# GPS layer (GCN, linear attention, expert FFN) on one NeuronCore: 16-bit count matrices, one clear per stored tile, V evictions ahead of the key store

## The chip, the cores and the metric

One Trainium2 chip, one of its NeuronCores. Engines are called PE (TensorE, matrix products), DVE (VectorE), ACT (ScalarE), POOL (GpSimd) and SP (SyncE, which here only issues transfers). The metric is the device time of one execution in microseconds (us), taken as the median of several runs. The kernel before takes 2583.36 us (2581.44 to 2583.81 in 3 runs).

## The reference

3125 nodes with 768 features and 50000 edges, float32. A transformer-like layer:

```python
xn = layernorm(x)
# two GCN convolutions:  out = D^-1/2 (A + I) D^-1/2 (h W^T) + b,  relu between
# A[dst, src] counts edges, D is the in-degree with the self loop
# linear attention over all nodes, 12 heads of 64, 256 random features:
#   q_p, k_p = exp(t @ rf^T - |t|^2 / 2) / 16 ;  kv = k_p^T v ;  out = q_p kv / (q_p . sum k_p)
#   then a projection, a residual on xn, layernorm with gamma and beta
x = x + gcn(gcn(xn)) + attention(xn)
x = x + ffn(layernorm(x))      # 8 experts of width 128, the larger index of the top 2 decides
```

## The kernel before, in words

The nodes are padded to 25 tiles of 128 rows, and these are taken in 5 chunks of 5 tiles. Products in near float32 accuracy are made of three float16 products (high times high, high times low, low times high), written by `mm_split` (L368 to L374, its matmuls all carry line L372).

**The counts.** The adjacency matrix with its counts is not given; the kernel builds it in device memory as two arrays of 3200 x 3200 cells (`cells[0]` and `cells[1]`, L98), here float32, 41 MB each. Each must be cleared first, tile by tile: `clear_tile` (L385) writes 128 x 3200 cells from a zero buffer in on-chip memory, 1600 KB in pieces of 640 elements, and 50 such transfers clear both. Then POOL adds the edges with 392 indirect accumulating transfers of 128 cells each (L711), alternately into the two arrays so that two can be under way. Its first batch of 14 needs only `cells[0]` cleared, the second batch on needs both (L716 to L724).

**Order of the work.** Everything that SP issues goes in a written order through one queue:

- *Prologue.* SP loads the first 5 tiles of x, the random features, 6 weight blocks of 768 KB and the edge lists (L466 to L491). After the normalised tiles are made, it stores each (`store_xn`, L475) and issues two clears behind each store, 10 in all (L497 to L499). Then it loads the first three x tiles of the next chunk (L500 to L501), waits for the edge keys from DVE, stores them (L503), waits for the store, and loads two blocks of keys copied to all partitions (`kb`, L506).
- *Stage 1*, per chunk c (L515 to L549 for SP, `chunk1` at L1681 for PE): PE makes V for 5 tiles, and K for 6 pairs of heads; each pair p is a unit in which exp of the features, sums of K and V and the degree counts are made. Unit number m = 6c + p. In each unit SP loads a key block as soon as DVE has finished its scan (L532 to L535), issues three clears (`CLEAR_FIRST`, `CLEAR_STEP`, L55, L536), stores an xn tile, loads x tiles, and stores and loads one weight block that ACT and DVE split into halves (`presplit_step`, L509; `presplit_hi` on ACT, L306; `presplit_lo` on DVE, L315). PE runs chunks 0 to 3 in a loop of two chunks per iteration, and chunk 4 behind it.
- *Stage 2* (attention for the queries) uses nothing of the counts. POOL's edge transfers run beside it.
- *Stage 3*: the first GCN product of all 25 tiles, then layer 1: for each of the 25 row tiles SP loads `cells[0]` (L596, L609) to `a_in`, POOL adds `cells[1]` to it with an accumulating transfer (L729) and adds the self loops to the diagonal block (L735), ACT makes the float16 high part (L972), DVE the low part (L1391, L1394), and PE multiplies (L1833). The halves are stored to `ahl_dram` for layer 2, which loads them again.
- *Stage 4*: layer 2, routing and the expert FFN.

**The start of stage 1.** PE makes V of tiles 0 and 1 into two PSUM slots. The third needs a slot back, which ACT gives when it has evicted the first (`activation` at L845). ACT first waits for three things:

```python
            act.wait_ge(consts, 2)
            act.wait_ge(vals_clear, 1)
            act.wait_ge(key_stored, 16)
```

`vals_clear` comes from DVE (L1166 to L1171): after the whole chain for the edge keys (L1144 to L1162) it waits until all 5 xn stores have landed (the buffers `vals` and `kv` lie on the same memory as the x tiles), and clears both. `key_stored` is the landing of the key store (the buffer `kh` that `cast_k`, L821, writes lies on the keys).

Of the kernel before, what the change touches and what calls it, by code (L numbers as in the profile page):

```python
# [15 lines left out]
F16 = mybir.dt.float16  # L16
I32 = mybir.dt.int32
ALU = mybir.AluOpType
# [36 lines left out]
CLEAR_FIRST, CLEAR_STEP = 10, 3  # L55
# [34 lines left out]
def build(nc, x, src_row, dst_row, src_col, dst_col, w_qkv, w_proj, b_proj, gamma, beta, rf_t,  # L90
          g1_t, b1, g2_t, b2, ffn_in, ffn_out, out):
    ctx = ExitStack()
    with ctx:
# [4 lines left out]
        cells = [dram(f"cells{k}", [CELLS, 1]) for k in range(2)]  # L98
# [13 lines left out]
        def at(off, *shape, dt=F32):  # L112
            n = int(np.prod(shape))
            if dt == F16:
                ap = arena[:, off:off + (n + 1) // 2].bitcast(F16)[:, 0:n]
            else:
                ap = arena[:, off:off + n]
                if dt != F32:
                    ap = ap.bitcast(dt)
            if len(shape) == 2:  # L120
                ap = ap.rearrange("p (a b) -> p a b", a=shape[0])
            if len(shape) == 3:
                ap = ap.rearrange("p (a b c) -> p a b c", a=shape[0], b=shape[1])
            return ap
# [5 lines left out]
        def small(*shape, dt=F32):  # L130
            n = int(np.prod(shape))
            n = (n + 1) // 2 if dt == F16 else n
            off = s_at[0]
            s_at[0] += n
            assert s_at[0] <= 53000
            return at(off, *shape, dt=dt)
# [5 lines left out]
        iota = small(P, dt=F16)  # L142
        earlier = small(G, G * P)
# [20 lines left out]


        kcol, idx_all, val_all = at(RX, ET), at(WST + 2304, NE, dt=I32), at(WST + 2304 + NE, NE)
        zeros = at(RT + 4 * 3840, 640)
        far = at(RT + 4 * 3840 + 640, SLOTS // P, dt=I32)
# [41 lines left out]
        a_in = [at(RT + NP * u, NP) for u in range(2)]  # L210
# [172 lines left out]
        zero_rows = zeros.rearrange("p (o f) -> p o f", o=1).to_broadcast([P, 5, 640])  # L383

        def clear_tile(eng, k, n):  # L385
            return eng.dma_start(cells_t[k][n].rearrange("p (a f) -> p a f", a=5), zero_rows)  # L386
# [77 lines left out]
        def _(sp):  # L464
# [25 lines left out]
            for i, a in enumerate((src_row, dst_row, src_col, dst_col)):  # L490
                sp.dma_start(eint[2 * i], a).then_inc(edges_in, 16)  # L491
            def clear(first, count):
# [4 lines left out]
            for n in range(TC):  # L497
                store_xn(n)
                clear(CLEAR_FIRST * n // TC, CLEAR_FIRST // TC)  # L499
            for j in range(3):  # L500
                load_x("seen", 1, j)  # L501
# [164 lines left out]
        def _(pool):  # L666
# [5 lines left out]
            made.link(nc.gpsimd.memset(zeros, 0.0))  # L672
            made.link(nc.gpsimd.affine_select(out=ident_end, in_=ident, compare_op=ALU.is_ge, fill=0.0,
                                              base=-(FIRST_LOOP % P), pattern=[[0, P]], channel_multiplier=1))
            made.link(nc.gpsimd.iota(iota, pattern=[[1, P]], base=0, channel_multiplier=0,
# [50 lines left out]
            for n in range(T):  # L726
                own = a_in[n % 2][:, n * P:(n + 1) * P]
                pool.wait_ge(a_ld[n % 2], 16 * (n // 2) + 16)
                pool.dma_start(a_in[n % 2], cells_t[1][n], accum_op=ALU.add, max_dma_last_dim=2 * NP)\  # L729
# [4 lines left out]
                else:  # L734
                    nc.gpsimd.tensor_tensor(own, own, ident_end if n == FIRST_LOOP // P else ident, ALU.add)\  # L735
                        .then_inc(loops, 1)
# [40 lines left out]
        def _(act):  # L777
# [60 lines left out]
            act.wait_ge(key_stored, 16)  # L838
            for c in range(C):
                more = c + 1 < C  # L840
                for t in range(TC):
# [9 lines left out]
                    if t == TC - 2:  # L851
                        cast_k(c, 0)
# [225 lines left out]
        def _(dve):  # L1078
# [64 lines left out]
            dve.wait_ge(consts, 2)  # L1143
            e = Chain(dve, dve_done, links(20))  # L1144
# [21 lines left out]
            dve.wait_ge(xn_st[0], 16 * 3)  # L1166
            dve.wait_ge(xn_st[1], 16 * 2)
            ch = Chain(dve, dve_done, links(2))
            ch.link(nc.vector.memset(kv, 0.0))
            ch.link(nc.vector.memset(vals, 0.0))  # L1170
            dve.sem_inc(vals_clear, 1)  # L1171
            dve.wait_ge(key_stored, 16)
# [869 lines left out]
```

## Time and profile before

| | |
|---|---|
| median of 3 runs | 2583.36 us |
| span of the profiled execution, first to last instruction | 2579.3 us |
| what lies around the span, median less span | 4.1 us |
| PE busy | 2372.9 us (92%) |
| DVE, ACT, POOL busy | 51%, 34%, 32% |
| moved by DMA | 474.24 MB |
| TensorE clock, mean of the span | 0.964 of full |

The profiled execution has no device time of its own beside the span. A group row reads: line, engine, operation, output and input, count, then busy time, mean length of one in ns, idle time of the engine before them and what ended most of it. "SPq" is the issue of a transfer by SP, of which the time is only that of the issue.

### The profile page before, as it was taken

The page shows a single profiled execution, that of the slowest core. Times are in us where ns is not written, and L with a number is a line of the kernel's source. Part 1 is how long each engine was busy: PE and PEld are TensorE (multiplying, and loading weights), DVE is VectorE, ACT ScalarE, POOL GpSimd, SP SyncE. Part 2 cuts the span into 40 slices and gives each one's busy share as a digit, 9 for nine tenths or more (in the row PEclk, how much of TensorE's full clock was granted, in tenths as well). Part 3 has the DMA queues.
Part 4 walks back from the last instruction along what each step waited for, and adds up shares of the span by engine and source line. Part 5 has one row for each costly group of instructions (what it writes and reads, how often), then busy time and mean ns, then how long its engine had stood idle before and what let it go on. Part 6 is the DMA issues. An engine that isn't in the chain of part 4 may idle for free.

```text
span 2579.3 us, 45374 instructions
## 1 busy us (share of the span) xinstructions
PE 2372.9 (92%) x16783; PEld 1607.5 (62%) x16783; DVE 1304.3 (51%) x2843; ACT 872.7 (34%) x1323; POOL 817.4 (32%) x565
## 2 busy tenths in 40 slices
PE   3899889999899999998899999999998899999576
PEld 2686768787666666665565566666664556666365
DVE  5464547564476766766313444544441334444444
ACT  2353436454474654745112222222220001111033
POOL 0002103656677777877610000000000000000265
PEclk9889899999899999999999999999998999999799
DMA  9698977664423233132543999999986655444287
GB/s 389 243 404 286 400 274 247 165 164 115 99 2 62 11 52 61 0 62 7 130 103 110 295 289 302 278 303 274 283 269 237 210 195 173 171 160 157 73 171 129
DMA packets 192199, 474.24 MB, mean 184 GB/s; under 512 B 74864, under 2 KB 81882, under 8 KB 182460
## 3 DMA queue, kind: packets, MB, share of 16 engines
q1 hardware_dynamic: 109996, 381.82, 40.6%
q0 software_dynamic: 71264, 61.03, 18.0%
q10 hardware_dynamic: 10800, 29.50, 3.0%
q8 instruction: 92, 1.51, 0.2%
q14 instruction: 47, 0.39, 0.0%
HBM read 266.99 MB, written 210.77 MB: 185 GB/s over the span
## 4 chain that ended last, share of the span: by engine, by line
PE 71%; ACT 8%; DVE 8%; DMA 6%; issue 4%; SPq 3%; POOL 0%; DVEq 0%; ACTq 0%; POOLq 0%
PE pair L1833 30%; PE pair L372 27%; PE pair L1665 4%; PE pair L1595 2%; PE pair L1645 2%; DVE arena L1297 2%; DVE arena L1299 2%; DVE arena L1303 2%; ACT arena L902 2%; DMA arena<-in_w_qkv 1%; DMA arena<-in_w_proj 1%; PE pair L1977 1%; PE pair L1964 1%; SPq L386 1%; DMA arena<-ahl_dram 1%
## 5 line engine op out<-in xcount | busy, mean ns | idle before, releaser
L372 PE MATMUL pair<-arena 128*128 128x384 f16 (+2 forms) x5760 | 912.9, 320 | 53.4 <-ACT arena L845 29.0
L711 POOL DMA_INDIRECT cells<-arena x392 | 653.5, 1667 | 626.6 <-DMA cells<-arena 501.1
L1833 PE MATMUL pair<-arena 128*128 128x384 f16 x4900 | 819.6, 328 | 27.2 <-DMA arena<-ahl_dram 12.9
L372 PEld LDWEIGHTS pair<-arena 128*128 128x128 f16 (+1 forms) x5760 | 569.5, 99 | 380.2 <-issue 57.3
L1833 PEld LDWEIGHTS pair<-arena 128*128 128x128 f16 x4900 | 475.6, 98 | 337.2 <-issue 14.6
L741 POOL DMA_INDIRECT slots<-arena x25 | 28.9, 1155 | 493.9 <-DVEq L1521 461.3
L1665 PE MATMUL pair<-arena 128*128 128x66 f32 x1200 | 165.3, 283 | 4.6 <-ACT arena L862 4.2
L1665 PEld LDWEIGHTS pair<-arena 128*128 128x128 f32 x1200 | 154.7, 201 | 13.2 <-ACT arena L862 11.0
L862 ACT ACTIVATE arena<-pair,arena 128x256 f32<-128x256 f32 x300 | 124.0, 473 | 60.9 <-PE pair L1645 58.3
L1764 PE MATMUL pair<-arena 128*128 128x320 f32 x480 | 135.2, 435 | 0.0
L1752 PE MATMUL pair<-arena 128*128 128x320 f16 x720 | 113.9, 303 | 19.7 <-DVEq L1306 15.4
L977 ACT ACTIVATE arena<-arena 128x768 f32<-128x768 f32 x25 | 23.4, 936 | 301.7 <-DVE arena L1400 301.7
L1466 DVE SCALAR_TENSOR_TENSOR arena<-pair,arena 128x768 f32<-128x768 f32 x25 | 25.4, 1017 | 195.0 <-PE pair L1833 195.0
L902 ACT ACTIVATE arena<-pair 128x640 f32<-128x640 f32 x120 | 80.7, 696 | 120.5 <-PE pair L1752 119.9
L729 POOL DMA_DIRECT2D arena<-cells x25 | 30.3, 1213 | 283.3 <-DMA arena<-cells 283.3
L1391 DVE TENSOR_TENSOR arena<-arena 128x3200 f16<-128x3200 f32 x25 | 87.3, 3492 | 58.4 <-ACT arena L972 58.4
L1764 PEld LDWEIGHTS pair<-arena 128*128 128x128 f32 x480 | 90.4, 192 | 34.9 <-issue 0.8
L1192 DVE SCALAR_TENSOR_TENSOR arena<-arena 128x128 f16<-128x128 f32 x392 | 109.2, 346 | 4.3 <-DVE arena L1120 4.3
L1752 PEld LDWEIGHTS pair<-arena 128*128 128x128 f16 x720 | 68.7, 99 | 59.5 <-issue 18.8
L735 POOL TENSOR_TENSOR arena<-arena 128x128 f32<-128x128 f32 x24 | 10.1, 421 | 293.2 <-DMA arena<-cells 293.2
L1037 ACT COPY arena<-pair 128x768 f16<-128x768 f16 x25 | 20.0, 799 | 228.4 <-DVE arena L1466 197.3
L1645 PE MATMUL pair<-arena 128*128 128x256 f16 x600 | 93.2, 290 | 0.0
(198 smaller groups left out, 2431.6 us busy)
## 6 DMA issues: line engine op xcount, KB each, us to landing
cells<-arena SPq DMA_DIRECT2D x50, 1600.0 KB, 16.6
arena<-cells SPq DMA_DIRECT2D x25, 1600.0 KB, 10.6
arena<-cells POOLq DMA_DIRECT2D x25, 1600.0 KB, 13.4
ahl_dram<-arena SPq DMA_DIRECT2D x25, 1600.0 KB, 14.1
arena<-ahl_dram SPq DMA_DIRECT2D x25, 1600.0 KB, 7.7
arena<-in_x SPq DMA_DIRECT2D x70, 384.0 KB, 5.2
arena<-key_dram SPq DMA_DIRECT2D x28, 896.0 KB, 5.9
split_w<-arena SPq DMA_DIRECT2D x32, 384.0 KB
```

The lines of the kernel that those rows point to most:

```text
L372: ins = nc.tensor.matmul(dst[half], left(k, a), right(k, b, half), start=start and n == 0, stop=stop and n == 2)
L711: nc.gpsimd.indirect_dma_start(cells[k], bass.IndirectOffsetOnAxis(ap=idx_all[:, m:m + 1], axis=0), val_all[:, m:m + 1], None, bounds_chec ...
L862: ins = nc.scalar.activation(kp_sb[q][:, h * M:(h + 1) * M], bank(4 + q)[:, h * M:(h + 1) * M], ACT.Exp, bias=knorm[:, p % 2, 2 * t + h:2 ...
L902: nc.scalar.activation(qp_sb[:, g, :].rearrange("p (a b) -> p a b", a=2), bank_pair(1 + s), ACT.Exp).then_inc(qp_free[s], 1)
L1192: nc.vector.scalar_tensor_tensor(out=junk[j % 2], in0=kb[p % 2][:, (j // G) * G * P:(j // G + 1) * G * P], scalar=kcol[:, bass.ds(m * EPU ...
L1297: cn.link(nc.vector.scalar_tensor_tensor(halves_of(ln_den[DH:P]), bank_pair(1 + s)[DH:P], 1e-6, halves_of(den[h][DH:P]), ALU.add, ALU.mult))
L1391: nc.vector.tensor_tensor(a_hl[u][:, 1, :], a_in[u], a_hl[u][:, 0, :], ALU.subtract).then_inc(counts_lo, 1)
L1645: ins = nc.tensor.matmul(bank(4 + n % 2)[:, h * M:(h + 1) * M], kh[p % 2][:, h, t * P:(t + 1) * P], weights, start=(h == 0 and m == 0), st ...
L1665: ins = nc.tensor.matmul(bank(6)[:, g * VW:(g + 1) * VW], kp_sb[n % 2][:, h * M + half * P:h * M + (half + 1) * P], vals[:, t, 2 * p + h, ...
L1752: ins = nc.tensor.matmul(pair[1 + s][:, b, 0:HW], w, rows[p % 2][:, h, b * HW:(b + 1) * HW], start=(n == 0), stop=(n == 2))
L1764: ins = nc.tensor.matmul(pair[1 + s][:, b, 0:HW], kvr[:, p, g, :], qp_sb[:, g, b * HW:(b + 1) * HW], start=(half == 0), stop=(half == 1))
L1833: ins = nc.tensor.matmul(pair[u][:, half, 0:HD], a[:, 0, s * P:(s + 1) * P], X[part][:, s, half * HD:(half + 1) * HD], start=(s == 0 and p ...
```

## The change

- `cells`, `zeros`, `a_in` and `val_all` become unsigned 16-bit. All counts are small whole numbers. A clear is now 800 KB in pieces of 1600 elements; the load of a count tile and the accumulating load are 800 KB each.
- One clear instead of two behind each stored tile: 5 in the prologue, and three per unit as before. So `cells[0]` is done with the clears of unit 6 (before: unit 4), and `cells[1]` with those of unit 14 (before: unit 13).
- The self loops are added through a float32 copy: three POOL operations in place of one.
- SP issues two of the x loads of chunk 1 at once, behind the edge lists, and the third behind the first xn store, in place of all three behind the last clear.
- DVE clears `kv` and the two last columns of each head in `vals` before the edge-key chain, not after it, and no longer the whole of `vals`.
- ACT waits for the key store only ahead of the first `cast_k`; DVE no longer waits for it.

```diff
-CLEAR_FIRST, CLEAR_STEP = 10, 3
+CLEAR_FIRST, CLEAR_STEP = 5, 3
-        cells = [dram(f"cells{k}", [CELLS, 1]) for k in range(2)]
+        cells = [dram(f"cells{k}", [CELLS, 1], U16) for k in range(2)]
+        loop, loop_end, own_f = small(P), small(P), small(P)
-        kcol, idx_all, val_all = at(RX, ET), at(WST + 2304, NE, dt=I32), at(WST + 2304 + NE, NE)
-        zeros = at(RT + 4 * 3840, 640)
+        kcol, idx_all, val_all = at(RX, ET), at(WST + 2304, NE, dt=I32), at(WST + 2304 + NE, NE, dt=U16)
+        zeros = at(RT + 4 * 3840, 1600, dt=U16)
-        a_in = [at(RT + NP * u, NP) for u in range(2)]
+        a_in = [at(RT + NP * u, NP, dt=U16) for u in range(2)]
...
-            return eng.dma_start(cells_t[k][n].rearrange("p (a f) -> p a f", a=5), zero_rows)
+            return eng.dma_start(cells_t[k][n].rearrange("p (a f) -> p a f", a=2), zero_rows)
...
                 sp.dma_start(eint[2 * i], a).then_inc(edges_in, 16)
+            for j in range(2):
+                load_x("seen", 1, j)
...
                 store_xn(n)
+                if n == 0:
+                    load_x("seen", 1, 2)
                 clear(CLEAR_FIRST * n // TC, CLEAR_FIRST // TC)
-            for j in range(3):
-                load_x("seen", 1, j)
             sp.wait_ge(key_made, 1)
...
-            made.link(nc.gpsimd.memset(zeros, 0.0))
+            made.link(nc.gpsimd.memset(zeros, 0))
+            made.link(nc.gpsimd.tensor_copy(loop, ident))
+            made.link(nc.gpsimd.tensor_copy(loop_end, ident_end))
...
-                pool.dma_start(a_in[n % 2], cells_t[1][n], accum_op=ALU.add, max_dma_last_dim=2 * NP)\
+                pool.dma_start(a_in[n % 2], cells_t[1][n], accum_op=ALU.add, max_dma_last_dim=NP)\
...
-                    nc.gpsimd.tensor_tensor(own, own, ident_end if n == FIRST_LOOP // P else ident, ALU.add)\
-                        .then_inc(loops, 1)
+                    pool.wait_ge(loops, n)
+                    made.link(nc.gpsimd.tensor_copy(own_f, own))
+                    made.link(nc.gpsimd.tensor_tensor(own_f, own_f, loop_end if n == FIRST_LOOP // P else loop, ALU.add))
+                    nc.gpsimd.tensor_copy(own, own_f).then_inc(loops, 1)
...
             act.wait_ge(vals_clear, 1)
-            act.wait_ge(key_stored, 16)
...
                     if t == TC - 2:
+                        if c == 0:
+                            act.wait_ge(key_stored, 16)
                         cast_k(c, 0)
...
             dve.wait_ge(consts, 2)
+            dve.wait_ge(xn_st[0], 16 * 3)
+            dve.wait_ge(xn_st[1], 16 * 2)
+            ch = Chain(dve, dve_done, links(2))
+            ch.link(nc.vector.memset(kv, 0.0))
+            ch.link(nc.vector.memset(vals[:, :, :, DH:VW], 0.0))
+            dve.sem_inc(vals_clear, 1)
             e = Chain(dve, dve_done, links(20))
...
             dve.sem_inc(kv_free, 1)
-            dve.wait_ge(xn_st[0], 16 * 3)
-            dve.wait_ge(xn_st[1], 16 * 2)
-            ch = Chain(dve, dve_done, links(2))
-            ch.link(nc.vector.memset(kv, 0.0))
-            ch.link(nc.vector.memset(vals, 0.0))
-            dve.sem_inc(vals_clear, 1)
-            dve.wait_ge(key_stored, 16)
```

## Rows read from the trace of the kernel before

**Rows 1.** The page: the chain that ended last, by engine.
```profile
PE 71%; ACT 8%; DVE 8%; DMA 6%; issue 4%; SPq 3%; POOL 0%; DVEq 0%; ACTq 0%; POOLq 0%
```
**Rows 2.** By chunk: PE, PEld, DVE, ACT, POOL busy (count), clock, DMA share, GB/s.
```profile
34.60:193.60 159.00, 129.20 (x960) 100.33 (x960) 83.57 (x277) 57.85 (x111) 0.00 (x0) 0.84 0.87 340
193.60:336.80 143.20, 124.97 (x964) 98.58 (x961) 74.47 (x263) 61.24 (x115) 23.49 (x14) 0.90 0.94 348
336.80:454.00 117.20, 116.51 (x960) 91.51 (x961) 73.00 (x259) 62.33 (x116) 26.82 (x16) 0.97 0.72 245
454.00:569.80 115.80, 114.92 (x961) 90.99 (x962) 75.06 (x261) 62.68 (x115) 68.38 (x41) 0.99 0.63 167
```
**Rows 3.** PE's waits, 45 to 345 us: in total, times, longest.
```profile
PE pair L372 <- ACT arena L845: 29.0, 2, 26.1
PE pair L1600 <- ACT arena L796: 10.4, 3, 4.9
PE pair L372 <- issue: 6.9, 1, 6.9
```
**Rows 4.** Order of time, 33 to 75 us: start, length, engine, line.
```profile
33.73 0.29 DVE L1146 CAST arena<-arena 128x256 f16<-128x256 f32 x1
34.69 14.34 PE L372 MATMUL pair<-arena 128*128 128x384 f16 x72 [3.80 <-DVE arena L297]
...
43.06 0.38 DVE L1161 TENSOR_SCALAR arena<-arena 128x420 f16<-128x420 int32 x1
...
61.08 1.38 DVE L1169 MEMSET arena<- 128x1584 f32 x1 [17.63 <-DMA xn_dram<-arena]
...
73.93 1.70 ACT L845 ACTIVATE arena<-pair,arena 128x768 f32<-128x768 f32 x2 [42.16 <-DMA key_dram<-arena]
...
75.12 25.34 PE L372 MATMUL pair<-arena 128*128 128x384 f16 x144 [26.08 <-ACT arena L845]
```
**Rows 5.** Windows as in rows 2: the prologue, then stretches of stage 1.
```profile
2.00:39.00 37.00, 12.49 (x74) 7.66 (x75) 31.62 (x51) 18.07 (x21) 5.09 (x22) 1.00 1.01 395
137.00:155.00 18.00, 18.00 (x171) 15.78 (x169) 14.13 (x46) 12.92 (x26) 0.00 (x0) 1.00 1.03 406
170.00:187.00 17.00, 17.00 (x99) 15.78 (x100) 9.00 (x30) 7.31 (x16) 0.00 (x0) 0.51 1.03 399
393.00:407.00 14.00, 14.00 (x121) 11.83 (x120) 10.86 (x41) 9.17 (x18) 0.00 (x0) 0.88 1.03 413
```
**Rows 6.** SP's queue: the clears of units 3 and 4.
```profile
155.17 10.20 SPq L386 DMA_DIRECT2D cells<-arena  x3
...
173.48 10.68 SPq L386 DMA_DIRECT2D cells<-arena  x3
```
**Rows 7.** Transfers issued from 104 to 206 us: KB each, median us to landing.
```profile
cells<-arena SPq DMA_DIRECT2D x18, 1600.0 KB, 16.7
arena<-in_w_qkv SPq DMA_DIRECT2D x5, 384.0 KB, 12.3
```
**Rows 8.** POOL, edge transfers and the first count tile of layer 1.
```profile
408.29 1.54 POOL L711 DMA_INDIRECT cells<-arena  x1 [102.56 <-DMA cells<-arena]
...
458.85 1.54 POOL L711 DMA_INDIRECT cells<-arena  x1 [2.01 <-DMA cells<-arena]
...
1293.40 1.55 POOL L711 DMA_INDIRECT cells<-arena  x1 [1.28 <-DMA cells<-arena]
...
1319.53 1.23 POOL L729 DMA_DIRECT2D arena<-cells  x1 [14.72 <-DMA arena<-cells]
```
**Rows 9.** Layer 1: the first count tile on ACT; then one tile from POOL to PE.
```profile
1384.43 2.85 ACT L972 CAST arena<-arena 128x3200 f16<-128x3200 f32 x1
...
1442.81 0.42 POOL L735 TENSOR_TENSOR arena<-arena 128x128 f32<-128x128 f32 x1 [12.25 <-DMA arena<-cells]
...
1449.68 0.19 DVE L1394 COPY arena<-arena 53x128 f16<-53x128 f16 x1
...
1465.83 4.39 PE L1833 MATMUL pair<-arena 128*128 128x384 f16 x26
```

More of the change, by code:

```diff
@@ L17 @@
 I32 = mybir.dt.int32
+U16 = mybir.dt.uint16
 ALU = mybir.AluOpType
@@ L113, in at @@
             n = int(np.prod(shape))
-            if dt == F16:
-                ap = arena[:, off:off + (n + 1) // 2].bitcast(F16)[:, 0:n]
+            if dt in (F16, U16):
+                ap = arena[:, off:off + (n + 1) // 2].bitcast(dt)[:, 0:n]
             else:
@@ L131, in small @@
             n = int(np.prod(shape))
-            n = (n + 1) // 2 if dt == F16 else n
+            n = (n + 1) // 2 if dt in (F16, U16) else n
             off = s_at[0]
@@ L163, in build @@
         pre_raw, pre_out = at(WST, 1032), at(WST + 1032, 2 * 1032, dt=F16)
-        kcol, idx_all, val_all = at(RX, ET), at(WST + 2304, NE, dt=I32), at(WST + 2304 + NE, NE)
-        zeros = at(RT + 4 * 3840, 640)
-        far = at(RT + 4 * 3840 + 640, SLOTS // P, dt=I32)
+        kcol, idx_all, val_all = at(RX, ET), at(WST + 2304, NE, dt=I32), at(WST + 2304 + NE, NE, dt=U16)
+        zeros = at(RT + 4 * 3840, 1600, dt=U16)
+        far = at(RT + 4 * 3840 + 800, SLOTS // P, dt=I32)
         kh = [at(RX + 1200 + CW * u, 2, CW, dt=F16) for u in range(2)]
@@ L380, in all_cleared @@
             eng.wait_ge(cleared[k], 16 * T)
-        zero_rows = zeros.rearrange("p (o f) -> p o f", o=1).to_broadcast([P, 5, 640])
+        zero_rows = zeros.rearrange("p (o f) -> p o f", o=1).to_broadcast([P, 2, 1600])
         def clear_tile(eng, k, n):
-            return eng.dma_start(cells_t[k][n].rearrange("p (a f) -> p a f", a=5), zero_rows)
+            return eng.dma_start(cells_t[k][n].rearrange("p (a f) -> p a f", a=2), zero_rows)
         chain_of, before_group, groups = {}, {}, [0, 0]
```

## The prediction

> **What bounds the kernel now.** I read the chain that ended last first: 71% of it is PE, 6% DMA, 3% SP's queue [rows 1]. So time is to be had where PE waits. Then the busy times cut at the borders of the chunks of stage 1 [rows 2]: chunks 2 and 3 take 117.2 and 115.8 us with PE busy for all but 1 us; chunk 0 takes 159.0 with PE busy for 129.2, chunk 1 143.2 with 125.0, and in these two the DMA engines are busy 87 and 94% of the time. The four chunks do the same work (960 matmuls). So some 42 and 26 us of the first two are stalls and slow clock, and both are rich in DMA. PE's waits name the largest piece: 26.1 us in one wait for ACT's V eviction, 2.9 in a second, 10.4 us for transposes, and one of 6.9 us with no releaser, where PE's loop goes back at 330 us [rows 3].
>
> In order of time [rows 4]: PE finishes V tiles 0 and 1 at 49.0 and stops until 75.1. ACT's first eviction, at 73.9, waited for the key store to land; that store waited behind the prologue's clears in SP's queue; and DVE, done with the edge keys at 43.4, idled 17.6 us until the xn stores had landed. From 2 to 39 us the queue moved 395 GB/s, in the units of chunk 0 about 400, with the DMA engines busy all the time [rows 5]: this is the full rate, and SP falls behind. The clears of unit 3 go out at 155.2, those of unit 4 at 173.5, 18.3 us apart [rows 6], where a unit of chunk 2 takes about 14 us.
>
> **Part by part.**
>
> *The first stall: 26.1 us.* The last xn store lands once all ahead of it is moved. Ahead of it are the weights (6 x 768 KB), 8 x tiles, 5 stores of 384 KB, 1.1 MB of edges and the rest, and now 4 clears of 800 KB: 14.3 MB, where 8 clears of 1600 KB made it 23 MB or more. At 395 GB/s from 2 us on that is 38 us; before, it was 61.1 [rows 4]. DVE reaches that wait at 33.7 (it now stands ahead of the edge chain), idles 5 us, clears `kv` in 1.4 and the two columns in an estimated 0.3, and frees ACT at about 40.5. V tile 0 is done near 43 (the 72 matmuls' 14.3 us fit 16 at 0.32 us, half of full speed, and 56 at 0.163), so its eviction runs at once, and PE passes 49.0 without a stop. Margin: DVE may be 6 us later.
>
> What is queued behind DVE's new wait is the edge chain, 9.7 us long (33.7 to 43.4). It ends at 50.3 in place of 43.4. The key store then meets an empty queue: I take 4 us for it, so `key_stored` is there at 54.5, and the key blocks (two of 896 KB, 4.6 us at 400 GB/s) at 61. `cast_k` needs `key_stored` only after V 2, V 3 and K 0, at 49.0 + 3 x 5.9 = 66.7: covered by 12 us. The x loads of chunk 1 (tiles 3 and 4) go out behind the key blocks and land near 62; statistics end near 65, before DVE is wanted at 68. Without this cover the same few us would come back.
>
> *No second cold start: 1.8 us.* After the stall PE took 25.3 us for 144 matmuls [rows 4]; at 0.163 us each these are 23.5.
>
> *The rest of chunk 0: 11.5 us.* From 75.1 to 193.6 are 118.5 us; the same part of chunk 2 is 117.2 less 12.0 for two V tiles, 105.2. Of the 13.3 too much 1.8 stand above. The rest is a wait of 3.2 us and a stretch from 170 to 187 at granted clock 0.51, half of full speed [rows 5], right behind that wait. Both come from late transfers: a weight block lands 12.3 us after its issue [rows 7], ACT and DVE wait for it in order, and the x tile behind it on DVE is late for PE's transposes. From 104 to 206 us, six units, 18 clears of 1.64 MB went out [rows 7], 29.5 of some 42 MB. Halved they leave 27.3 MB, 4.6 MB a unit, 11.4 us at 400 GB/s, against 14 us of PE's work. SP no longer falls behind. A unit of chunk 2 that ran at DMA share 1.03 kept PE busy all its 14.0 us [rows 5], so short bursts are harmless.
>
> The Trainium skill speaks against this step: "DMA: Bandwidth & Descriptors" (Bandwidth) wants transfers of 1 MiB or more for 75% of peak, and a clear falls from 1.6 MB to 0.8. It has 341 GB/s at 1 MB; as an estimate from it a unit would take 13.4 us or more, and the queue would hardly keep up (the first rival's case). The trace disagrees: the queue of rows 5 held transfers of 384 to 1600 KB and moved 400.
>
> *Chunk 1: 24 us.* It takes 143.2; chunk 2 takes 117.2; the difference is 26.0. In it are the waits of 2.9, 7.2 of the 10.4, 6.9 at the loop's end, and another stretch at half speed. The 6.9 us have no releaser in the trace; they fell in full DMA traffic, and I read them as PE waiting for its instructions to be fetched behind it. I leave 2 us of them (ends 0 and 6.9; nearer to 0, since the queue will be busy four fifths of the time and not all of it).
>
> *Chunk 2: 0.* It now holds nine clears of 0.8 MB where it had four of 1.6.
>
> *Edge transfers: 0.* Their second batch waits for the clears of unit 14, not 13: 14 us later beside PE, less 6 for the shorter landing. So they start at 408.3 - 63 + 8 = 353 and need 885 us for 377 steps [rows 8], 2.35 each: the last at 1238. The first count tile is ready 26 us later (1293.4 to 1319.5 before): 1264, and ACT wants it at 1384.4 [rows 9] - 63 = 1321. Cover 57 us.
>
> *Layer 1: 0.* The count tile for the next row tile is finished on DVE at 1449.9, and PE takes it up at 1465.8 [rows 9]: 16 us of cover. Three POOL operations for one of 0.42 us [rows 9] cost about 1.3 us more with their waits, two transfers of half the bytes give more than that back. Ends: 0, or a loss only if the accumulating load of 16-bit cells took over 16 us more than now. The two extra copies in the prologue and the longer zero buffer (under 1 us) end before SP is wanted at 13.9.
>
> Sum: 26.1 + 1.8 + 11.5 + 24 = 63.4. From the span of 2579.3 that is 2516; with the 4.1 us around it, against the median of 2583.4, **2520 us**.
>
> **Rivals.**
> 1. *Traffic still lags in chunks 0 and 1.* 16-bit transfers move fewer bytes per second, or the late landings have another cause. Then the 35.5 us of the two chunks come by half or less, 0 to 18: 2537 to 2555. For: the clears stay 54% of a unit's bytes. Against: chunks 2 and 3. Chance 0.13.
> 2. *The first stall moves to the xn stores.* If the last store lands not at 38 but near 50, DVE frees ACT 6 us too late and PE stops there; the edge chain, the keys and `cast_k` follow 6 us later inside their cover. 2526 to 2530. Chance 0.07.
> 3. *The edge transfers become the bound* (slower than before). Accumulating into 2-byte cells may land later, and each array's transfers wait for one another. Price: from 408.3 to 458.9 there are 17 steps [rows 8], 2.97 us each, mostly waiting. At that pace for all 377 the last is at 353 + 1120 = 1473, the first tile ready at 1499, 178 late against 1321: 2520 + 178 = 2698. It decides from 2.50 us a step (57/377 more); from 2.67 on the kernel is slower than before. Against: that stretch had much other traffic, and later steps follow POOL's own 1.5 us. Chance 0.03.
> 4. *The change does not free V*: `vals_clear` comes as late as before. Only a wrong reading of the order would do it; 2520 + 26 = 2546. Chance 0.01.
>
> **How the numbers follow.** Forecast 0.76. A measurement of this kernel tells some 0.2% (5 us) from no change. Range: downward the 6.9 us fully gone, chunk 3's pace for chunks 0 and 1, and a little elsewhere, 2508; upward half of the two chunks' gain lost and some of rival 2, 2541. That leaves out the worse part of rival 1 and rival 3. Faster: all but rival 3, 0.96; same 0.01; slower 0.03.
>
> **What would show it.** Right: V evictions from about 43 us on, no PE gap at 49; the last xn store landing near 38, DVE's `kv` clear right behind it; clears of one chunk at the pace of PE's units, 14 us, with weight blocks landing in 4 to 8 us; chunks 0 and 1 near 120 us each; PE at full clock throughout; POOL's second batch from about 353. Wrong: chunks 0 and 1 still over 130 us, a gap at 49, edge steps over 2.5 us, or a longer row tile in layer 1 than now.

## The result and the profile after

The change made the kernel faster: **2524.94 us** median (2520.66 to 2531.73 in four runs) against 2583.59 for the kernel before on the same chip, ratio 0.9779 with a 95% interval of 0.976 to 0.9797. The forecast was 2520.0 in a range of 2508 to 2541. The profiled execution took 2527.59 us, its span is 2525.8, so 1.8 us lie around a span. I had taken 4.1 for that, the median of before less the span of one execution. With 1.8 around it that execution took some 2581.1 us, 2.3 under its median, and the profiled one after is 2.7 above its own. So the spans lie 53.5 us apart and the medians 58.6.

The page of the kernel after: the engines, the DMA total, and the chain by engine, which answers to [rows 1].

```profile
span 2525.8 us, 45448 instructions
...
PE 2350.2 (93%) x16783; PEld 1590.9 (63%) x16783; DVE 1261.0 (50%) x2843; ACT 870.3 (34%) x1323; POOL 866.3 (34%) x615
...
DMA packets 172999, 392.22 MB, mean 155 GB/s; under 512 B 74864, under 2 KB 81882, under 8 KB 166460
...
PE 77%; DVE 8%; ACT 8%; issue 4%; DMA 3%; SPq 0%; POOL 0%; DVEq 0%; ACTq 0%; POOLq 0%
```

SP's queue has left the chain (3% to 0%), DMA has halved in it (6% to 3%), and 82 MB fewer are moved (474.24 less 392.22): the clears of both arrays are 41 MB smaller, and so are the loads of their tiles.

By chunk, against [rows 2] and the first of [rows 5] (length, then PE, PEld, DVE, ACT, POOL busy with counts, granted clock, DMA share, GB/s):

```profile
34.60:152.40 117.80, 117.17 (x960) 91.74 (x960) 80.97 (x279) 58.42 (x112) 0.00 (x0) 0.99 0.74 263
152.40:274.50 122.10, 114.67 (x962) 91.27 (x960) 74.81 (x264) 61.49 (x115) 17.14 (x10) 0.97 0.85 291
274.50:391.70 117.20, 116.21 (x949) 91.09 (x950) 72.32 (x258) 61.27 (x115) 25.72 (x15) 0.97 0.68 214
2.00:39.00 37.00, 12.56 (x74) 7.67 (x75) 26.82 (x39) 18.06 (x21) 6.44 (x24) 1.00 1.01 392
```

Chunk 0 fell from 159.0 to 117.8 us, chunk 1 from 143.2 to 122.1, and chunk 2 stayed. PE's waits from 30 to 300 us, which answer to [rows 3]:

```profile
PE pair L374 <- issue: 7.0, 1, 7.0
PE pair L374 <- DVE arena L299: 3.8, 1, 3.8
PE pair L1674 <- ACT arena L872: 0.9, 3, 0.4
```

The wait for the V eviction is gone. The one without a releaser, at the end of PE's loop, is still there. In order of time, against [rows 4], [rows 6] and [rows 8]:

```profile
34.63 36.63 PE L374 MATMUL pair<-arena 128*128 128x384 f16 x216 [3.80 <-DVE arena L299]
...
39.95 1.38 DVE L1157 MEMSET arena<- 128x1584 f32 x1 [6.20 <-DMA xn_dram<-arena]
...
41.41 0.16 DVE L1158 MEMSET arena<- 128x120 f32 x1
...
43.17 0.90 ACT L853 ACTIVATE arena<-pair,arena 128x768 f32<-128x768 f32 x1 [11.47 <-PE pair L374]
...
51.52 0.33 SPq L508 DMA_DIRECT2D key_dram<-arena  x1
...
53.47 0.80 SPq L511 DMA_DIRECT2D arena<-key_dram  x2
...
120.60 2.07 SPq L388 DMA_DIRECT2D cells<-arena  x3
...
134.69 2.13 SPq L388 DMA_DIRECT2D cells<-arena  x3
...
274.55 36.14 PE L374 MATMUL pair<-arena 128*128 128x384 f16 x216 [7.00 <-issue]
...
358.97 1.55 POOL L718 DMA_INDIRECT cells<-arena  x1 [64.58 <-DMA cells<-arena]
...
1243.60 1.55 POOL L718 DMA_INDIRECT cells<-arena  x1 [0.30 <-issue]
...
1259.24 1.23 POOL L736 DMA_DIRECT2D arena<-cells  x1 [6.64 <-POOLq L740]
```

PE runs through the first 216 matmuls of V without a stop. DVE frees ACT at 41.6, and ACT evicts the first V at 43.2, as soon as PE has it: the releaser is now PE. The clears of two units go out 14.1 us apart and take 2.1 us to issue, not 10, so SP no longer waits for room in its queue. The second batch of edge transfers starts at 359.0, the last goes out at 1243.6, 2.35 us a step as before, and the accumulating load of the second count tile goes out at 1259.2.

**Where the time went.** The same event in both traces, in us:

| event | before | after | gained so far |
|---|---|---|---|
| chunk 2 begins | 336.85 | 274.55 | 62.3 |
| stage 3, first product | 1246.20 | 1185.03 | 61.2 |
| stage 4, first product of layer 2 | 1976.48 | 1915.24 | 61.2 |
| end of the span | 2579.3 | 2525.8 | 53.5 |

Stage 1 gave nearly what the forecast sums up, the middle of the kernel took 1.1 us, and layer 2 gave 7.7 us back. There PE waits for count tiles of `ahl_dram`. The waits of PE on it in stage 4 (in total, times, longest), first before, then after:

```profile
PE pair L1833 <- DMA arena<-ahl_dram: 12.9, 2, 8.8
```

```profile
PE pair L1842 <- DMA arena<-ahl_dram: 19.8, 2, 11.5
```

The chain of each shows the transfer behind the second of these waits, before and after, from its issue to its landing:

```profile
2055.65 20.71 DMA arena<-ahl_dram
```

```profile
1993.71 28.12 DMA arena<-ahl_dram
```

It is the load of a count tile that SP issues right behind 14 weight blocks for the expert FFN. With the same transfers ahead of it, in the same order, it landed 7.4 us later. After, in windows as above, from the time of its issue on:

```profile
1994.00:1998.00 4.00, 4.00 (x44) 2.82 (x43) 2.93 (x8) 1.00 (x2) 0.00 (x0) 1.00 0.82 73
...
2010.00:2014.00 4.00, 0.46 (x3) 0.07 (x1) 1.02 (x1) 0.00 (x0) 0.00 (x0) 1.00 0.83 55
...
2018.00:2022.00 4.00, 0.05 (x1) 0.06 (x2) 0.00 (x0) 0.00 (x0) 0.00 (x0) 0.50 1.01 419
2022.00:2026.00 4.00, 4.00 (x21) 2.56 (x22) 1.27 (x3) 0.80 (x1) 0.00 (x0) 0.51 0.71 298
```

And before, in the two windows that answer to the first and second of these, and in the one where PE goes on:

```profile
2056.00:2060.00 4.00, 4.00 (x45) 2.77 (x44) 2.93 (x8) 1.00 (x2) 0.00 (x0) 1.00 0.82 209
2072.00:2076.00 4.00, 0.40 (x3) 0.01 (x1) 1.02 (x1) 0.00 (x0) 0.00 (x0) 1.00 0.94 165
2076.00:2080.00 4.00, 3.52 (x22) 2.26 (x23) 1.53 (x4) 0.80 (x1) 0.00 (x0) 0.69 0.99 408
```

The DMA engines show as busy in both, and yet move 73 and 55 GB/s after where they moved 209 and 165 before. When PE goes on at 2022 its granted clock is 0.51, its lower level (1.2 GHz), for another 4 us; before, it was 0.69 in the 4 us with the shorter wait. That clock costs little more than before: from the end of the wait to the routing products that close the row tile are 6.0 us after and 5.8 before. The two waits for count tiles are 6.9 us longer in sum, and the whole stretch from the end of the first to the end of the second takes 64.0 us in place of 56.5. That is 7.5 of the 7.7 us. No line that the change touches runs in this stage.

### The profile page after: what moved, and what is told of

Same layout as the page of the kernel before. It is cut to its first block, busy times and chain, and to the rows that moved or that the text cites. A ratio compares the mean times of both kernels' runs of the same rounds, so it can differ in the third digit from the quotient of the medians.

```text
span 2525.8 us, 45448 instructions
## 1 busy us (share of the span) xinstructions
PE 2350.2 (93%) x16783; PEld 1590.9 (63%) x16783; DVE 1261.0 (50%) x2843; ACT 870.3 (34%) x1323; POOL 866.3 (34%) x615
## 2 busy tenths in 40 slices
DMA packets 172999, 392.22 MB, mean 155 GB/s; under 512 B 74864, under 2 KB 81882, under 8 KB 166460
## 4 chain that ended last, share of the span: by engine, by line
PE 77%; DVE 8%; ACT 8%; issue 4%; DMA 3%; SPq 0%; POOL 0%; DVEq 0%; ACTq 0%; POOLq 0%
PE pair L1842 31%; PE pair L374 30%; PE pair L1674 4%; PE pair L1654 2%; PE pair L1604 2%; DVE arena L1306 2%; DVE arena L1308 2%; DVE arena L1312 2%; ACT arena L912 2%; DMA arena<-ahl_dram 1%; PE pair L1986 1%; PE pair L1663 1%; PE pair L1973 1%; ACT arena L896 1%; PE pair L1773 1%
## 5 line engine op out<-in xcount | busy, mean ns | idle before, releaser
L374 PE MATMUL pair<-arena 128*128 128x384 f16 (+2 forms) x5760 | 906.2, 319 | 25.4 <-SPq L363 12.8
L1842 PE MATMUL pair<-arena 128*128 128x384 f16 x4900 | 819.2, 328 | 34.5 <-DMA arena<-ahl_dram 19.8
L1674 PE MATMUL pair<-arena 128*128 128x66 f32 x1200 | 157.9, 275 | 4.8 <-ACT arena L872 4.3
L1674 PEld LDWEIGHTS pair<-arena 128*128 128x128 f32 x1200 | 146.6, 192 | 13.8 <-ACT arena L872 12.0
L1475 DVE SCALAR_TENSOR_TENSOR arena<-pair,arena 128x768 f32<-128x768 f32 x25 | 25.4, 1018 | 195.3 <-PE pair L1842 195.3
L1409 DVE SCALAR_TENSOR_TENSOR arena<-pair,arena 128x768 f32<-128x768 f32 x25 | 25.4, 1018 | 183.8 <-PE pair L1842 183.8
L1773 PEld LDWEIGHTS pair<-arena 128*128 128x128 f32 x480 | 90.5, 192 | 35.0 <-issue 0.8
L1604 PE MATMUL pair<-arena 128*128 128x128 f16 x984 | 71.8, 224 | 23.4 <-DMA arena<-hl_dram,arena 16.6
```

What stands on the lines that cost most here:

```text
L374: ins = nc.tensor.matmul(dst[half], left(k, a), right(k, b, half), start=start and n == 0, stop=stop and n == 2)
L1604: ins = nc.tensor.transpose(dst[:, k * P:(k + 1) * P], part[:, k * P:(k + 1) * P], ident)
L1674: ins = nc.tensor.matmul(bank(6)[:, g * VW:(g + 1) * VW], kp_sb[n % 2][:, h * M + half * P:h * M + (half + 1) * P], vals[:, t, 2 * p + h, ...
L1773: ins = nc.tensor.matmul(pair[1 + s][:, b, 0:HW], kvr[:, p, g, :], qp_sb[:, g, b * HW:(b + 1) * HW], start=(half == 0), stop=(half == 1))
L1842: ins = nc.tensor.matmul(pair[u][:, half, 0:HD], a[:, 0, s * P:(s + 1) * P], X[part][:, s, half * HD:(half + 1) * HD], start=(s == 0 and p ...
```

## The experiments

Each ran beside the kernel before on the same chip, and each ratio is against those runs. Three groups shared one set of them: the first repeat and the three edits that take the change apart (before: 2582.88 us), the four edits that follow from these (2584.37), and the second repeat with the two beside it (2586.55). The last edit had its own (2585.33).

**Is the give-back chance?** The changed kernel again, without an edit.

> The changed kernel as it stands, once more. In its profiled execution PE waited 11.5 us for a count tile (ahl_dram) in layer 2, where the kernel before waited 4.1, and its four times lie 11 us apart where those of before lie 3 apart. Theory: that wait is a matter of chance (14 FFN weight loads stand ahead of the tile in SP's queue), so another execution of the same kernel shows another wait, and its span differs by just that. Rival: the wait is a lasting part of the change; then it is 11 to 12 us again. Both: median 2525, chunk 0 117.8 us, chunk 1 122.1.

Measured: 2529.14 us (2525.01 to 2531.29), ratio 0.9788 (0.9764 to 0.9811). PE's waits for `ahl_dram` came to 19.2 us, the load landed after 25.4. A second repeat, later:

> The changed kernel a third time, on the same chip as the next two. PE's waits for count tiles in layer 2 were 19.8 and 19.2 us in its two profiles (18.1 and 18.8 in two others with 16-bit cells). Theory (place in memory): 18 to 20 us again. Rival (chance): anything from 12 to 20. Both: median 2525 to 2529.

Measured: 2529.78 us (2528.66 to 2534.03), ratio 0.9782 (0.9766 to 0.9799), waits 20.5 us, landing 28.9. Three profiles of the kernel after: 19.8, 19.2, 20.5. The second of the two waits, which the first expectation speaks of, was 11.5, 11.0 and 12.3. It is not chance.

**The order and the waits alone, with float32 cells.**

```diff
-        cells = [dram(f"cells{k}", [CELLS, 1], U16) for k in range(2)]
+        cells = [dram(f"cells{k}", [CELLS, 1]) for k in range(2)]
-        zeros = at(RT + 4 * 3840, 1600, dt=U16)
+        zeros = at(RT + 4 * 3840, 640)
-        a_in = [at(RT + NP * u, NP, dt=U16) for u in range(2)]
+        a_in = [at(RT + NP * u, NP) for u in range(2)]
```

(and back to float32 in `val_all`, the clears, the accumulating load and the self loops).

> The change without its 16-bit cells: five float32 clears in the prologue, the new order and waits. Theory (bytes): ahead of the last xn store stand 17.5 MB, it lands near 46 us, so PE's wait of 26 us is gone but for 1 us (27 us of the gain), while chunks 0 and 1 stay full of traffic and keep their 35 us: 2556, and chunk 2 is hit too, since it now holds nine full clears: up to 2562. Rival (the early wait was the cause of the later ones as well): chunks 0 and 1 near 118 and 122 us, 2525.

Measured: 2572.12 us (2567.43 to 2579.22), ratio 0.9959 (0.9946 to 0.9972), 10 to 16 us slower than expected. Its chunks 0 to 2, in windows as above:

```profile
35.20:174.50 139.30, 127.07 (x960) 98.95 (x960) 81.29 (x279) 57.65 (x111) 0.00 (x0) 0.89 0.89 340
174.50:312.90 138.40, 124.80 (x964) 98.50 (x961) 74.28 (x263) 61.54 (x115) 14.44 (x9) 0.89 0.92 348
312.90:441.90 129.00, 123.56 (x966) 96.84 (x967) 74.09 (x262) 62.36 (x116) 25.23 (x16) 0.92 0.82 288
```

And, in order of time, PE behind its third V tile:

```profile
51.48 8.84 PE L374 MATMUL pair<-arena 128*128 128x384 f16 x43 [2.45 <-ACT arena L851]
```

The first stall is nearly gone (2.4 us), and chunk 2 begins at 312.9, 24 us earlier than before. But chunk 2 itself takes 129.0 where it took 117.2 [rows 2]: it now holds nine clears of 1.6 MB where it had four, and the traffic that was taken out of the prologue slows it by 12 us. With float32 cells, moving clears only moves the lag, which the expectation had missed. That nine clears in place of four cost nothing in chunk 2 of the changed kernel is owed to the halved cells.

**The type alone**: 16-bit cells, with the old order, 10 clears in the prologue and the old waits.

```diff
-CLEAR_FIRST, CLEAR_STEP = 5, 3
+CLEAR_FIRST, CLEAR_STEP = 10, 3
+            act.wait_ge(key_stored, 16)
-                        if c == 0:
-                            act.wait_ge(key_stored, 16)
```

(with the clears of `kv` and the whole of `vals` back behind the edge keys, and the x loads behind the last clear).

> Only the 16-bit cells: ten clears in the prologue, x loads, clears of vals and kv and the waits for the key store as before. Theory (bytes): the last xn store lands near 46, DVE has cleared vals at 52, the key store has landed by then, PE stops for 4 to 6 us in place of 26; chunks 0 and 1 as in the changed kernel: 2528 to 2532, so the type alone brings over 50 of the 59 us. Rival (order and waits carry the first 26 us): a stop of over 15 us, 2545 or more.

Measured: 2532.76 us (2532.38 to 2533.99), ratio 0.9805 (0.9784 to 0.9826). Its two rows at the first stall:

```profile
45.96 1.38 DVE L1175 MEMSET arena<- 128x1584 f32 x1 [2.27 <-DMA xn_dram<-arena]
...
54.54 5.71 PE L374 MATMUL pair<-arena 128*128 128x384 f16 x26 [5.17 <-ACT arena L851]
```

The type alone takes 26.1 us of stall down to 5.2, because the stores and the key store stand in one queue behind half the bytes, and it brings 50 us. The time is 0.8 us above the expected range and the stop inside it. The new order and waits add 3.6 us against the repeat that ran beside it, which the two intervals do not separate; the profiles do, by the 5.2 us of stall.

**The waits alone**: the kernel before, with DVE's clears ahead of the edge keys and ACT's wait for the key store ahead of the first `cast_k`; DVE no longer waits for that store.

```diff
-            act.wait_ge(key_stored, 16)
+                        if c == 0:
+                            act.wait_ge(key_stored, 16)
             dve.wait_ge(consts, 2)
+            dve.wait_ge(xn_st[0], 16 * 3)
+            dve.wait_ge(xn_st[1], 16 * 2)
```

> The kernel before with the waits alone moved (vals and kv cleared ahead of the edge chain, the key store awaited at the first cast_k); float32 cells, ten clears. Theory: DVE now waits for the last xn store, still at 61 us, frees ACT at 63, PE stops for 15 us in place of 26: 2572 to 2574, chunks 0 and 1 otherwise as before. Rival (the key store was the whole wait): PE stops for under 3 us, 2557.

Measured: 2571.21 us (2568.31 to 2573.52), ratio 0.9952 (0.9935 to 0.9969), 0.8 us under the expected range.

```profile
61.27 1.38 DVE L1148 MEMSET arena<- 128x1584 f32 x1 [26.86 <-DMA xn_dram<-arena]
...
64.25 25.02 PE L372 MATMUL pair<-arena 128*128 128x384 f16 x144 [15.55 <-ACT arena L844]
```

DVE now idles 26.9 us for the same landing, at 61.3 us (61.1 in [rows 4]), and 15.6 us of the stall stay: a wait that is moved ends no earlier than the transfer it is for.

The parts do not add. Waits alone bring 12 us, order and waits with float32 11, the type 50, all of them 54 to 59: in part they remove the same stall.

**What delays the count load of layer 2?** In the runs that came before this one, PE's two waits for `ahl_dram` in stage 4 were in sum 12.9 (before), 14.3 and 13.7 us with float32 cells, and 18.1 to 19.8 with 16-bit cells. The arrays are no longer in use by then. But with half the bytes each, everything in device memory that is allotted behind them may lie elsewhere. So: 16-bit cells, in arrays of the old size in bytes.

```diff
-        cells = [dram(f"cells{k}", [CELLS, 1], U16) for k in range(2)]
+        cells = [dram(f"cells{k}", [2 * CELLS, 1], U16)[0:CELLS, :] for k in range(2)]
```

> The changed kernel, but each 16-bit count array is the first half of an array of twice the length, so that both take as many bytes of device memory as before and the tensors behind them keep their old places. In the three executions with 16-bit cells PE waits 10.1 to 11.5 us for a count tile in layer 2, behind the 14 FFN weight loads, in the three with float32 cells 4.1 to 6.0. Theory (place in memory): the wait falls back to 4 to 6 us, the median to 2518 to 2521. Rival (it is not where the tensors lie): 10 to 12 us again, 2525 to 2529.

Measured: 2522.89 us (2521.36 to 2526.2), ratio 0.9762 (0.974 to 0.9784), 1.9 us above the range of the theory. The second wait is 5.4 us, inside it. PE's waits in stage 4:

```profile
PE pair L1842 <- DMA arena<-ahl_dram: 13.6, 2, 8.3
```

And the two windows that answer to the first two of the kernel after:

```profile
1995.80:1999.80 4.00, 4.00 (x44) 2.78 (x43) 2.86 (x6) 1.00 (x2) 0.00 (x0) 1.00 0.65 89
2011.80:2015.80 4.00, 0.73 (x5) 0.22 (x3) 1.02 (x1) 0.00 (x0) 0.00 (x0) 1.00 1.04 166
```

The second is again like before (166 GB/s for 165); the first is not (89, near the 73 of the kernel after), though the load landed after 22.0 us. So the low rate of the first window does not mark the slow case by itself.

And once more, beside the second repeat of the kernel after:

> The arrays of the old byte size again: its one profile had 13.6 us of waits for count tiles in layer 2, where the float32 kernels have 12.9 to 14.3. Theory (place in memory): 13 to 14.5 us again, and a median some 4 to 6 us under the changed kernel's of the same chip. Rival (chance): waits anywhere from 12 to 20, no difference in the median.

Measured: 2525.61 us (2521.47 to 2531.88), ratio 0.9772 (0.9754 to 0.9789).

```profile
PE pair L1842 <- DMA arena<-ahl_dram: 14.4, 2, 8.7
```

In the profiles the 6 us are back both times. In the medians this version is 4.2 us under the repeat that ran beside it, with ranges that overlap, so in the time of whole executions it is likely and not settled. The length of stage 4 in the profiles, from its first product to the end of the span, says more: 602.8 to 605.2 us in the five profiles with arrays of the old byte size (before, both runs with float32 cells, both of this version), and 608.8 to 612.5 in the six with arrays of half and all 14 loads at once. The wait follows the size of arrays that stage 4 does not touch. Whether that acts through the addresses of `ahl_dram` or of the weights, and why one place is slower, no trace here shows.

**The jump of PE's loop, written out.**

```diff
-            with pe.Fori(0, (C - 1) // 2) as i:
+            for i in range((C - 1) // 2):
```

> The changed kernel with PE's loop over chunks 0 to 3 written out, no jump. PE stood for 7.0 us at the end of chunk 1 in the changed kernel and for 6.9 in the one before, though the traffic there has halved. Theory (the price of the jump itself): without it PE stands under 1 us, 2518 to 2520. Rival (something else at that place, as a semaphore that comes late): 7 us again, 2525.

Measured: 2514.15 us (2513.44 to 2514.65), ratio 0.9724 (0.9704 to 0.9745), 4 us under the range of the theory. The first V products of chunk 2:

```profile
266.04 34.31 PE L374 MATMUL pair<-arena 128*128 128x384 f16 x216
```

No wait stands ahead of it, chunk 2 begins 8.5 us earlier than in the kernel after, and its first 216 matmuls take 34.3 us in place of 36.1. That makes 10 us: the wait, 1.8 behind it, and 1.5 ahead of it. In the two profiles as a whole it is more: chunk 4 begins 12.9 us earlier (495.1 for 508.0), and the spans differ by as much. The jump accounts for the wait of 7.0 and the slow start of 1.8. The other 4 us lie mostly in stretches of some 4 us at half the granted clock with PE busy all the time, which chunks 1 to 3 of the kernel after show at 258, 354 and 470 us and the written-out one only once (at 372). Other profiles show them at other places, so these 4 us are not shown to be the jump's.

**The FFN weight loads spread** over the first three row tiles of layer 2 (5, 5, 4), in place of 14 at once.

```diff
-                if isinstance(n, int) and n == 2:
-                    for k in range(K):
-                        sp.dma_start(w_in(k), split_dram[FFN_AT + k]).then_inc(ffn_ready, 16)
-                    for x8 in range(NX):
-                        sp.dma_start(w_out(x8), split_dram[FFN_AT + K + x8]).then_inc(ffn_ready, 16)
+                if isinstance(n, int):
+                    for w in range(5 * n, min(5 * n + 5, K + NX)):
+                        sp.dma_start(w_in(w) if w < K else w_out(w - K), split_dram[FFN_AT + w]).then_inc(ffn_ready, 16)
```

> The changed kernel with the 14 loads of FFN weights spread over three row tiles of layer 2 (5, 5 and 4) in place of all behind the third. Theory: the count tile behind them is no longer late, the wait of 11 us and the slow clock after it (some 3 us) go: 2511 to 2514. Rival (these loads are slow wherever they stand, and stop PE three times a little): 2520 or more.

Measured: 2515.15 us (2514.04 to 2523.95), ratio 0.9728 (0.9707 to 0.9748), 1 us over the expectation. PE's waits for `ahl_dram` in stage 4 fell from 19.8 to 12.1 us:

```profile
PE pair L1840 <- DMA arena<-ahl_dram: 12.1, 2, 7.1
```

Stage 4 took 604.9 us. The profiled execution was the slowest of the four (2523.95, the others at most 2516.04), so it does not show all that the median gained.

**Both of these**, which is the fastest version found:

> Both edits at once, the loop written out and the FFN loads spread. Theory: the two gains add, about 7 and 13 us: 2504 to 2507. Rival: one of them is not there, 2512 or more.

Measured: 2500.92 us (2500.59 to 2506.36), ratio 0.9674 (0.9653 to 0.9694), 3 us better than expected: 24 us under the kernel after (2524.94, on another chip). Here too the profiled execution was the slowest of the four; its stage 4 took 603.6 us, with waits of 13.0.

**All three**, with the old array sizes too:

> Loop written out, FFN loads spread, arrays of the old byte size. With the loads spread, PE's waits for count tiles were already 12.1 and 13.0 us with the new sizes. Theory (place matters only for the block of 14 loads): no further gain, 2500 to 2502. Rival (place matters for all of layer 2's loads): 2495 or less.

Measured: 2503.48 us (2501.46 to 2505.62), ratio 0.9681 (0.9665 to 0.9697). PE's waits in stage 4:

```profile
PE pair L1840 <- DMA arena<-ahl_dram: 7.5, 1, 7.5
```

The median, 1.5 us over the range of the theory, shows no further gain. The profile speaks against the reason given for it: the second wait, 5.0 and 5.9 us in the two profiles with spread loads and half arrays, is gone, and stage 4 took 597.2 us where it took 604.9 and 603.6. So the size of the arrays still matters with the loads spread, in the one execution that was profiled; why the median does not follow is open, since the other executions have no trace.

**Is the wait at the jump a fetch behind the traffic?** In the kernel after, chunk 1 as a whole had a DMA share of 0.85, the wait itself 1.01. Its 7.0 us, after:

```profile
267.55:274.55 7.00, 0.00 (x1) 0.01 (x1) 1.41 (x3) 0.04 (x1) 2.26 (x1) 0.78 1.01 381
```

The last edit takes the clears of unit 11 away from it:

```diff
-                    clear(CLEAR_FIRST + CLEAR_STEP * m, CLEAR_STEP)
+                    if m != 2 * PAIRS - 1:
+                        clear(CLEAR_FIRST + CLEAR_STEP * (m - (m >= 2 * PAIRS)), CLEAR_STEP)
```

> The changed kernel with one edit: the unit at the end of chunk 1 (unit 11) issues no clears, and every later unit issues those of the unit before it, so the last clears go out in unit 15 instead of 14. In all profiles so far the DMA engines were busy 98 to 104% of the time during PE's wait at the end of its loop (267.6 to 274.6 us in the changed kernel), and two packets of an instruction queue lie in it. Without unit 11's three clears (2.5 MB) the queue should run empty before the wait begins and stay so until SP issues the x loads of the next chunk, 2 to 3 us later. Theory A, PE's instructions are fetched behind the other traffic: the wait falls from 7 or 8 us to between 2 and 4.5, chunk 2 begins near 271, and the time is 3 to 6 us under the changed kernel. Theory B, the jump has a fixed price: the wait stays at 6 to 8 us, chunk 2 begins at 274 to 276, the time is the same within 2 us. Under both the edge transfers start up to 14 us later and stay hidden.

Measured: 2525.69 us (2524.19 to 2527.72), ratio 0.9775 (0.9752 to 0.9798). PE's first row behind the jump, in order of time, with the wait in brackets:

```profile
271.45 36.44 PE L374 MATMUL pair<-arena 128*128 128x384 f16 x216 [5.04 <-issue]
```

The window of that wait:

```profile
266.40:271.40 5.00, 0.02 (x1) 0.00 (x0) 1.50 (x3) 0.83 (x1) 0.00 (x0) 0.76 0.62 182
```

And what the DMA engines moved in it, in 40 slices of 0.125 us, with the instruction queue (packets, MB, share of all 16 engines):

```profile
GB/s 573 344 189 172 246 115 1 58 0 58 0 57 0 57 0 0 0 0 0 0 0 0 123 418 319 418 393 369 369 393 271 123 172 197 270 295 344 344 295 295
...
q8 instruction: 2, 0.03, 4.1%
```

The queue ran nearly empty for 2 us in the middle, two packets of instructions fell into the wait, and it still lasted 5.0 us. That lies between the two theories (2 to 4.5, or 6 to 8). Ten profiles at full traffic gave 5.8 to 8.3 us. So most of the price, about 5 us, is there with little traffic; that traffic adds up to 3 on top is suggested by this one profile and not more. What the 5 us are is open. Both instruction packets lie in the first 0.9 us of the wait (until 267.3 us); from 268.2 to 269.2 the DMA engines moved next to nothing, and PE went on only at 271.45. In three of the ten profiles at full traffic a single packet lies in the wait, not two. So the wait is the jump's, as the written-out loop shows, but it does not end with the landing of a packet that the trace shows. The time did not move, and the clock still fell (36.4 us for the 216 matmuls, 34.3 without the jump).

## Why the prediction was right, and where it was off

- *The first stall, 26.1 us*: right. DVE's `kv` clear was forecast at 38 to 39 and came at 39.95 behind the xn stores; ACT was free at 41.6 (40.5), and the first eviction ran at 43.17 (43). The prologue moved 392 GB/s (395). The key store went out at 51.5, the key blocks at 53.5 (54.5), and no wait for `cast_k` appeared. The type alone would have done 21 of the 26.
- *No second cold start, and the rest of chunk 0, 1.8 + 11.5 us*: right in size, for the three terms of chunk 0 together. Chunk 0 took 117.8 us for 159.0, 41.2 less, where the three terms sum to 39.4. Weight blocks landed after 5.2 us for 12.3 [rows 7], inside the 4 to 8 that were named, and the clears after 9.2 for 16.7. The transfers issued from 64 to 150 us, after (KB each, median us to landing):

```profile
cells<-arena SPq DMA_DIRECT2D x16, 800.0 KB, 9.2
...
arena<-in_w_qkv SPq DMA_DIRECT2D x6, 384.0 KB, 5.2
```

- *The rule weighed against it*, transfers of 1 MiB or more for 75% of peak ("DMA: Bandwidth & Descriptors", Bandwidth, in the Trainium skill), did not decide. The clears in the prologue were now 800 KB each, its other large transfers 384 to 768 KB, and it moved 392 GB/s with DMA share 1.01. With it fell the first rival: chunks 0 and 1 came by 41 and 21 us, not by half.
- *Chunk 1, 24 us*: 21.1 came. **The step that failed** is "I leave 2 us of them": the 6.9 us at the loop's end were sized by the traffic, and 7.0 stayed. It is a term of the sum that was mis-sized, 2 for 7.0. Two things were wrong in it. The queue would be busy four fifths of the time, but the wait falls where SP had just issued a unit's clears and where the next chunk's x loads follow, with DMA share 1.01; an average over the chunk said nothing of that. And traffic is not most of the price: with clears out of the way 5.0 us stayed. The far end of my own range for this term, 6.9, was the measured one. The total is off by only 2.9 us because chunk 2 of before, the 117.2 us that it was measured by, holds 1.6 us of slow start behind the same jump (35.9 us for its first 216 matmuls, 34.3 without a jump ahead): without its 7.0 us of wait chunk 1 took 115.1. By the Trainium skill ("Runtime: NRT & Kernel Launch", Instruction fetch mechanics) a taken branch whose target is not among the loaded instructions waits for a DMA fetch. The wait's absence in the written-out loop agrees; that it went on for 4 us behind the last instruction packet, with little traffic, the fetch alone does not explain.
- *Full clock throughout*, one of the signs: only in part. The granted clock was 0.99, 0.97 and 0.97 in chunks 0 to 2, and it fell to 0.50 for some 4 us in each of chunks 1 to 3 with PE busy all the time and no wait of over 1 us just ahead. The unit of chunk 2 that the prediction calls harmless had it too: its row in [rows 5] has PE busy for all 14.0 us, and a granted clock of 0.88. A stretch of 17 us at half speed, as before at 170 us, was not there any more. That it went with the late transfers is as forecast; that every slow stretch comes from a wait is not so.
- *Chunk 2, 0*: right, 117.2 for 117.2. The experiment with float32 cells shows what hid it: with nine clears of the old size it is 129.0.
- *Edge transfers, 0*: right. Second batch at 359 (353), last at 1243.6 (1238), 2.35 us a step; ACT's first use of a count tile came at 1322.9 (1321). The row at 1319.5 that the forecast took for the first tile is the second's; the first goes out at 1303.5 there and at 1251.3 after, so the cover is larger than was said. The third rival, slower steps on 2-byte cells, did not occur.
- *Layer 1, 0*: right. From stage 3 to stage 4 both kernels take the same, 730.3 and 730.2 us (1246.20 to 1976.48, 1185.03 to 1915.24).
- *Layer 2* was not in the sum at all, and took 7.7 us back, on a path that no step of the change touches. It was not foreseeable from the trace of before, which shows no addresses. What could have been seen there are the two waits for `ahl_dram`, 8.8 and 4.1 us, the second behind the 14 loads: a place with no cover, where anything that delays a transfer costs at once.
- *The sum*: 63.4 were forecast, 62.3 were there when chunk 2 began. Of the difference between 2520 and the profiled 2527.6, 1.1 us is the first stage, 1.1 the stretch to layer 2, 7.7 layer 2, less 2.3 for what lies around the span. The last is the slip of the 4.1 us. It does not touch the forecast as a forecast of the median (2583.4 less 63.4 is 2520 too), which was 4.9 us under the 2524.94 measured: the terms of stage 1 came within 1.1 us in sum, in part by luck, with 1.8 more in chunk 0 and 2.9 less in chunk 1, and the main miss is the term for layer 2 that was not there.

## What to carry to other kernels

Where one queue carries stores that an engine waits for and bulk traffic that nobody waits for, halve the bytes of the bulk first: here it was worth 50 us, and the finer order of clears and waits 4 on top of it (12 without it). Do not price a stall by the mean traffic of its stage, nor by traffic at all before it has been taken away once: PE's wait at its loop jump kept 5.0 of 7.0 us. After a change of array sizes, look also at the uncovered transfers of stages that the change does not touch.

## What the hardware showed beyond the forecast

- The low part of the counts on DVE became nearly twice as fast. Lines that read one tile, before and after (ns: min, median, max):

```profile
L1391 DVE TENSOR_TENSOR arena<-arena x25: 3491/3493/3493, 1387.3 to 1915.9; 128x3200 f16<-128x3200 f32 x25
```

```profile
L1400 DVE TENSOR_TENSOR arena<-arena x25: 1824/1825/1826, 1325.8 to 1854.2; 128x3200 f16<-128x3200 uint16 x25
```

  The Trainium skill ("VectorE: DVE Perf Modes", What auto-detection actually checks) has two results a cycle where every tensor is 16-bit and contiguous; the rows agree, with unsigned counts and float16 mixed. It was off the path: layer 1 gained nothing by it. ACT's copy of the same tile stayed at 2.86 us.
- The jump of PE's loop costs 5.0 us of wait with DMA share 0.62, 5.8 to 8.3 with 0.99 or more, and about 2 more in the clock after it.
- A load behind 14 others landed after 20.7 to 22.6 us with count arrays of the old size in bytes and after 23.9 to 28.9 with arrays of half; in the kernel after the DMA engines stood as busy for 0.82 and 0.83 of two windows of it while they moved 73 and 55 GB/s. The granted clock was 0.50 at the end of PE's 11.5 us wait and 1.00 again from 2026 us on.
- Accumulating transfers into 2-byte cells kept the pace of those into 4-byte cells, 2.35 us a step.
